# Graph attention over 8192 nodes: two edges packed in a byte before the adjacency is transposed, the packing by GpSimd, the unpacking by ScalarE, the row of neighbour terms in PSUM

## The reference

```python
h  = relu(layernorm(x))                     # x: 8192 x 128, float32
Wh = h @ W                                  # W: 128 x 128
f1 = Wh @ a[:128];  f2 = Wh @ a[128:]
e  = leaky_relu(f1[:, None] + f2[None, :], negative_slope=0.2)
e  = where(adj == 0, -inf, e)               # adj: 8192 x 8192, int32, about 0.2% ones
x + softmax(e, axis=1) @ Wh                 # float32
```

## Time and profile before

| | us |
|---|---|
| median of 3 runs (lowest, highest) | 870.19 (869.23, 870.61) |
| profiled execution, its span | 872.21, 870.5 |
| PE busy, DVE busy | 841.6 (97%), 766.2 (88%) |
| POOL busy, ACT busy | 137.0 (16%), 104.8 (12%) |
| transfers: mean rate | 87 GB/s written |

### The profile page before, as it was taken

How to read it: one execution, slowest core, us unless ns; L and a number is a source line. 1 busy time by engine, 2 the same in 40 slices (tenths; PEclk the granted TensorE clock), 3 DMA queues, 4 the chain that set the end, 5 groups by cost and what they waited for, 6 DMA issues and landing times.

```text
span 870.5 us, 23030 instructions
## 1 busy us (share of the span) xinstructions
PE 841.6 (97%) x9481; PEld 773.6 (89%) x9481; DVE 766.2 (88%) x1326; ACT 104.8 (12%) x286; POOL 137.0 (16%) x262
## 2 busy tenths in 40 slices
PE   3899999999999999999999999999999999999995
PEld 3788999999999999999999999999999999999995
DVE  4899898998989898898989889898989889898985
ACT  4788700000000000000000000000000000000000
POOL 3111111111111111111111111101110111111000
PEclk9999999999999999999999999999999999999998
DMA  9995699988998889888988998898889889988300
GB/s 219 113 107 52 59 112 87 94 92 80 95 91 90 83 91 95 81 92 87 97 83 90 91 85 92 81 103 83 90 83 94 92 81 94 93 90 82 48 2 15
DMA packets 43275, 75.95 MB, mean 87 GB/s; under 512 B 4720, under 2 KB 6896, under 8 KB 43248
## 3 DMA queue, kind: packets, MB, share of 16 engines
q0 software_dynamic: 38400, 67.13, 81.3%
q1 hardware_dynamic: 4432, 8.39, 2.9%
q10 hardware_dynamic: 416, 0.07, 0.0%
HBM read 272.70 MB, written 4.19 MB: 318 GB/s over the span
## 4 chain that ended last, share of the span: by engine, by line
PE 91%; DVE 6%; ACT 1%; DMA 1%; issue 1%; ACTq 0%; DVEq 0%
PE acc L275 50%; PE acc L279 26%; PE stage L264 13%; DVE wt_ring L620 3%; PE stage L237 1%; DVE stats L556 1%; DMA a_sb<-in_L_gnn_a_dram 1%; PE stage L224 1%; DVE pairs L611 1%; PE stage L252 1%; DVE xn L593 0%; ACT xn L399 0%; ACT wh L414 0%; DVE packed L603 0%; DVE xm L726 0%
## 5 line engine op out<-in xcount | busy, mean ns | idle before, releaser
L620 DVE SCALAR_TENSOR_TENSOR wt_ring<-row,packed,stage 128x512 f32<-128x512 uint8 (+1 forms) x1024 | 695.3, 742 | 74.9 <-PE acc L279 69.1
L275 PE MATMUL acc<-pairs,wt_ring 128*128 128x258 f16 x4096 | 720.2, 274 | 0.4 <-DVE wt_ring L620 0.2
L279 PE MATMUL acc<-pairs,wt_ring 128*128 128x129 f16 x4096 | 698.4, 219 | 0.0
L275 PEld LDWEIGHTS acc<-pairs,wt_ring 128*128 128x128 f16 x4096 | 396.2, 97 | 55.4 <-DVE wt_ring L620 0.4
L279 PEld LDWEIGHTS acc<-pairs,wt_ring 128*128 128x128 f16 x4096 | 399.5, 98 | 4.9
L178 POOL DMA_DIRECT2D masks<-in_adj_dram x252 | 133.2, 529 | 664.7 <-PE stage L264 635.7
L264 PE MATMUL stage<-ident,masks 128*128 128x128 f32 x1024 | 155.3, 275 | 2.0 <-ACT fin L483 2.0
L264 PEld LDWEIGHTS stage<-ident,masks 128*128 128x128 f32 x1024 | 108.7, 141 | 6.0 <-ACT fin L483 2.3
L513 ACT ACTIVATE fin<-acc 128x258 f32<-128x258 f32 x64 | 24.7, 386 | 730.2 <-PE acc L275 730.2
L237 PE MATMUL stage<-wx,ht 128*128 128x130 f32 x128 | 23.5, 311 | 0.7 <-ACT ht L408 0.7
L434 ACT ACTIVATE tmp<-wh,tmp 128x128 f32<-128x128 f32 x64 | 20.4, 390 | 0.4
(11 more groups left out here) (51 smaller groups left out, 80.1 us busy)
## 6 DMA issues: line engine op xcount, KB each, us to landing
masks<-in_adj_dram POOLq DMA_DIRECT2D x256, 256.0 KB, 8.8
out_dram<-xm SPq DMA_DIRECT2D x16, 256.0 KB, 2.1
xm<-in_x_dram SPq DMA_DIRECT2D x3, 1024.0 KB, 15.7
xm<-in_x_dram SPq DMA_DIRECT2D x1, 768.0 KB, 6.5
xm<-in_x_dram SPq DMA_DIRECT2D x1, 256.0 KB, 3.0
wx<-in_L_gnn_W_dram ACTq DMA_DIRECT2D x1, 64.0 KB, 3.2
a_sb<-in_L_gnn_a_dram ACTq DMA_DIRECT2D x1, 1.0 KB, 6.5
```

The lines of the kernel that those rows point to most:

```text
L275: return nc.tensor.matmul(acc[:, r, 0:2 * E1], wtv[:, w, r, 1, :], pairv[:, t, :, 0:E1], start=st, stop=end)
L279: return nc.tensor.matmul(acc[:, r, 0:E1], wtv[:, w, r, 0, :], pairv[:, t, 0, 0:E1], start=False, stop=False)
L620: nc.vector.scalar_tensor_tensor(out=wt_ring[:, t % NW, :], in0=e_row, scalar=packed[:, t, 1:2], in1=marks[:, k, :], op0=ALU.max, op1=ALU. ...
```

## The change

Rows 2 and 3 of each partition are multiplied by 200 and added to rows 0 and 1, so that one byte holds two edges (0, 1, 200 or 201). Only two blocks are then transposed per unit. The parts:

- **GpSimd** does, for each unit, `second` (the multiplication, on 128 x 2 x 256 16-bit words) and `mix` (the addition, on 128 x 2 x 128 32-bit words, which waits for `second` by a semaphore). It also takes over `scaled` and the second half of `normalise` in the first group, and `sums` and `outputs` of each group. Its loop is written out flat; it is ahead of PE by four to eight units.
- **ScalarE** does `unpack` for each unit: the bytes in PSUM times 1.28 plus 0.1, written as 16-bit integers into the ring `marks` of four units, so that the two bytes of each are the two edges. It also does `divided` (four 128 x 128 scalings) per group. `keep_row` is gone.
- **VectorE** reads E from PSUM (`stage`, bank 1 or 3) and the edges from SBUF (`marks`). `finish` is gone but for one reciprocal per group. It copies four columns of E for the next group into `e_next`.
- **TensorE** spreads E once per group, after unit 2, into the bank that is free, and transposes two units ahead into banks 0 and 2 in turn (before three ahead, over four banks).
- Loads: a chunk's rows 0 and 1 are loaded again when it is transposed, rows 2 and 3 when they are mixed. In the first group the loads of chunks 1 to 3 stand behind `second` and `mix` of units 0 to 3.

```diff
+            def mix(u):
+                c, k = u // KC % NC, u % KC
+                if k == 0 and u >= KC:
+                    pool.wait_ge(adj_loaded[c], (u // UN + (1 if c else 0)) * 2 * 16)
+                pool.wait_ge(s["second_pool"], u + 1)
+                sl = slice(k * P, (k + 1) * P)
+                nc.gpsimd.tensor_tensor(edges4[:, c, 0, :, sl], edges4[:, c, 0, :, sl], edges4[:, c, 1, :, sl],
+                                        ALU.add).then_inc(s["mixed"], 1)
+            def second(u):
...
+                nc.gpsimd.tensor_scalar(twos[:, c, 1, :, sl], twos[:, c, 1, :, sl], SECOND, None, ALU.mult
+                                        ).then_inc(s["second_pool"], 1)
+            def load_second(n):
+                pool.wait_ge(s["mixed"], (n - NC + 1) * KC)
...
+            def load_first(n):
+                pool.wait_ge(s["transposed"], (n - NC + 1) * KC)
...
+            def sums(q):
+                pool.wait_ge(s["acc_free"], (q + 1) * PACK)
...
+            for u in range(KC):
+                second(u)
+                mix(u)
+            for c in range(1, NC):
+                load_rows(c)
+            load_second(NC)
+            for b in range(UN):
+                if b % KC == 2:
+                    load_first(NC + b // KC)
+                if b + 1 < NQ:
+                    scaled(b + 1)
+                if b + 4 < NQ:
+                    normalise(b + 4)
+                second(b + KC)
+                mix(b + KC)
+                if b % KC == KC - 1:
+                    load_second(NC + 1 + b // KC)
+            for n in range(NC - 1, NQ * NC - 2):
+                if NC <= n < NQ * NC - NC:
+                    load_first(n + NC)
+                for k in range(KC):
+                    second((n + 2) * KC + k)
+                    mix((n + 2) * KC + k)
+                if n + 2 + NC < NQ * NC:
+                    load_second(n + 2 + NC)
+                if n >= NC and n % NC == 0:
+                    sums(n // NC - 1)
+                if n >= NC and n % NC == 2:
+                    outputs(n // NC - 1)
-                for r in range(PACK):
+                pe.wait_ge(s["mixed"], u + 1)
+                for r in range(2):
+                    mm = nc.tensor.transpose(stage[:, bank, r * P:(r + 1) * P], words[:, c * PACK + r, kk * P:(kk + 1) * P],
+                                             ident[:])
                 mm.then_inc(s["transposed"], 1)
+            def group(q, bank):
+                for b in range(UN):
+                    pe.wait_ge(s["marked"], q * UN + b + 1)
+                    transposes(b % 2 * 2, (b + 2) % UN, q * UN + b + 2)
                     unit(q * UN + b, b, q)
+                    if b == 2:
+                        pe.wait_ge(s["weighted"], q * UN * PACK)
+                        pe.wait_ge(s["e_ready"], q + 2)
+                        spread(bank)
+            def unpack(bank, u, b):
+                act.wait_ge(s["transposed"], u + 1)
...
+                nc.scalar.activation(split[:, b % MR, :].rearrange("p (s w) -> p s w", s=PACK),
+                                     stage[:, bank, 0:BANK // 2].bitcast(U8).rearrange("p (w s) -> p s w", s=PACK),
+                                     ACT.Copy, scale=SPLIT, bias=ABOVE).then_inc(s["marked"], 1)
-                marks = stage[:, bank, :].bitcast(U8).rearrange("p (w s) -> p s w", s=PACK)
+                edges = marks[:, b % MR, :].rearrange("p (s w h) -> p s h w", s=PACK, h=2)
+                e_row = stage[:, bank, :].rearrange("p (h k) -> p h k", h=2)
                 for k in range(PACK):
                     t = b * PACK + k
-                    nc.vector.scalar_tensor_tensor(out=wt_ring[:, t % NW, :], in0=e_row,
-                                                   scalar=packed[:, t, 1:2], in1=marks[:, k, :],
+                    nc.vector.scalar_tensor_tensor(out=wtq[:, t % NW], in0=e_row,
+                                                   scalar=packed[:, t, 1:2], in1=edges[:, k],
                                                    op0=ALU.max, op1=ALU.mult).then_inc(s["weighted"], 1)
```

More of the change, by code:

```diff
@@ L64, in gat_kernel @@
     NW = 8
+    MR = 4
     HALF = PACK // 2
@@ L88, in gat_kernel @@
         pairs = sb("pairs", [P, NB, 2 * WC], F16)
-        row = sb("row", [P, N], F32)
+        marks = sb("marks", [P, MR, CHUNK], U8)
         wt_ring = sb("wt_ring", [P, NW, BANK], F32)
@@ new lines, in normalise @@
+            def normalise(g):
+                pool.wait_ge(s["ln_ready"], batch_of(g) + 1)
+                pool.wait_ge(s["xt_ready"], g - 1)
+                for r in range(HALF, PACK):
+                    t = g * PACK + r
+                    ins = nc.gpsimd.tensor_scalar(xn[:, g % 2, r * P:(r + 1) * P], xm[:, g, r * P:(r + 1) * P],
+                                                  small[:, 5, t:t + 1], small[:, 6, t:t + 1], ALU.mult, ALU.add)
+                ins.then_inc(s["xn_pool"], 1)
@@ L189, in _, with outputs, load_rows @@
+            def outputs(q):
+                pool.wait_ge(s["fin_scaled"], q + 1)
+                y = xm[:, q, :].rearrange("p (r k) -> p r k", r=PACK)
+                nc.gpsimd.tensor_tensor(y, fin[:, :, 0:Fo], y, ALU.add).then_inc(s["rows_done"], PACK)
+            def load_rows(c):
                 pool.wait_ge(x_loaded[c + 1], 16)
@@ L191, in _ @@
                     load(0, c, r)
-            with pool.Fori(1, NQ) as q:
-                for c in range(NC):
-                    pool.wait_ge(s["transposed"], (q - 1) * UN + (c + 1) * KC)
-                    for r in range(PACK):
-                        load(q, c, r)
+            for u in range(KC):
[27 more added lines that the diff above has]
+                    outputs(n // NC - 1)
+            outputs(NQ - 2)
             pool.wait_ge(s["flag_ready"], 1)
@@ L309, in _ @@
             features(0, 1)
-            spread(0)
-            transposes(0, 0, 0, first=True)
+            transposes(0, 0, 0)
+            pe.wait_ge(s["e_ready"], 1)
+            spread(1)
             features(1, 0)
@@ L485, in _ @@
             for b in range(UN):
-                if b + 1 < NQ:
-                    scaled(b + 1)
+                if b + 1 < UN:
+                    unpack(0, b + 1, b + 1)
                 if b + 3 < NQ:
@@ L627, in first_weights, with next_group @@
                 if b == 0:
[L628 to L629 removed]
+                    dve.wait_ge(s["rowp_ready"], 1)
+                dve.wait_ge(s["marked"], b + 1)
                 if b >= 2:
                     dve.wait_ge(s["used"], b - 1)
[L632 removed]
+                weights(1, b)
+            def next_group(q):
+                dve.wait_ge(s["rowp_ready"], q)
+                nc.vector.tensor_copy(e_next[:], packed[:, bass.ds(q * PACK, PACK), 0]).then_inc(s["e_ready"], 1)
             nc.vector.memset(cst[:, 0:1], float(math.log(SCALE))).then_inc(s["cst_ready"], 1)
@@ L706, in _ @@
             nc.vector.tensor_scalar(lim[:, 1:2], low[:], -1.0, None, ALU.mult).then_inc(s["limits_ready"], 1)
-            dve.wait_ge(s["row_ready"], NQ)
-            with dve.Fori(1, NQ) as q:
-                rows(q)
+            with dve.Fori(0, (NQ - 2) // 2) as p:
+                rows(p * 2 + 1, 3)
+                rows(p * 2 + 2, 1)
+            rows(NQ - 1, 3, more=False)
             dve.wait_ge(s["limits_turned"], 1)
```

219 lines of the change are left out of this document (119 added, 100 removed).

## The result

| | before | after |
|---|---|---|
| median (lowest, highest), 4 runs each | 870.34 (869.23, 870.61) | 928.24 (925.82, 931.66) |
| ratio, 95% interval | | 1.0671 [1.0634, 1.0708] |
| profiled execution, its span | 872.21, 870.5 | 931.66, 930.0 |

The forecast was 827 us, the range 814 to 868, and faster had 0.86. The time lies above even the upper bound that the GpSimd rival gave (924 us).

A forecast was written before the change was run, and what follows sets the result against it. PE's instruction list was taken as the bound, with the DVE circle level with it: 870.5 us less 44.1 for groups 1 to 15, first group 0, gives 826.4, with half a microsecond for the tail 827 us; range 814 to 868.

The forecast's parts named there:

- the GpSimd rival: GpSimd's queue of packing and load issues becomes the bound above 2.93 us per unit; 924 us at 3.35; chance 0.24.
- GpSimd's price: GpSimd's work per unit: `second` 0.82 us, `mix` 0.82, with loads, wait, `sums` and `outputs` 2.64 us in all.
- upper bound of 2.19: Highest GpSimd cost considered, 2.19 ns per element from the select on 128 elements, giving 3.35 us per unit.
- margin of 0.29: GpSimd's forecast 2.64 us per unit against PE's 2.93, taken to fit by 10%.
- 240 c: Time of the later groups if GpSimd is the bound and a unit there takes c us.
- the sign: First sign of GpSimd as bound: DVE's reciprocal waiting for `sums`, forecast to end at 15.5 us, wanted at 17.6.
- The first group: Net change of the first group taken as 0, between -5 and +12 us; losing more than gaining had chance 0.06.
- The late start: In the first group, loads behind packing put `high_part(1)` at about 37.7 us, 8 late, 5 to 6 us lasting.
- A pass: First-group pass on DVE: 4.94 us to 4.4, 0.5 saved on 12 passes and some on the last four, 8 us.
- The rival of GpSimd and DVE blocking each other: DVE instructions with two SBUF tiles wait for GpSimd, 13 us, 840 us; weights, one SBUF tile, not held; chance 0.1.
- PE's list: PE's own instructions: two transposes fewer, 2.906 us per unit, and `spread` 0.44 us, 46.94 us per group against 50.02.
- the circle with DVE: DVE and PE waiting on each other across units: 2.908 us per unit, slack zero, no cost at today's DVE durations.

The follow-up runs named there:

- e6: The kernel after with PE's fourteen middle groups written out instead of looped, all else as after: 899.45 us, ratio 1.0341.
- e5: e1 with PE's fourteen middle groups written out, no jump back: 841.41 us, ratio 0.9662.
- e9: e5 with loads of chunks 1 to 3 ahead of the packing of units 1 and 2, and `scaled(1)` on ScalarE: 834.10 us, ratio 0.959.
- e8: e5 with loads of chunks 1 to 3 ahead of packing units 1 and 2, `scaled(1)` on ScalarE, `second` on ScalarE from unit 8: 832.66 us.
- e3: The kernel after with VectorE's reciprocal after unit 9 instead of 6 and the scalings after unit 11 instead of 8: 893.88 us, ratio 1.0258.
- e7: The kernel before with PE's loop body made two groups long, same instructions: 896.11 us, ratio 1.0290.
- e1: The kernel after with `second` moved from GpSimd to ScalarE from unit 20 on, six units ahead: 878.33 us, ratio 1.0090.

## Why the prediction was wrong

By medians, from after back to the forecast, in this order: PE without the long loop body -28.8 (e6); `second` off GpSimd -58.0 (e5); the start of the first group -7.3 (e9); `second` off GpSimd in the first group -1.4 (e8). That is 95.6 of the 101.2 us between 928.2 and 827. The other 5.7 us are in point 5. The shares depend on the order: the loop body was worth 37 us once GpSimd was out of the way.

1. **GpSimd's price, the step that failed most.** The prediction took 0.10 us fixed and 1.4 ns per element read, and so 0.82 us for `second`. It is 1.50 us, 2.9 ns per element, above even the upper bound of 2.19. `mix` on 512 elements read was 0.73 (0.82 forecast), `sums` 1.54 + 1.10 (2.36), `outputs` 1.20 (1.53). So of the computing instructions only the `tensor_scalar` was put too low, and it stood 256 times: 0.68 us per unit, against a margin of 0.29 (2.93 - 2.64). The rows used were of other instructions (memset, select) of at most 128 elements. The Trainium skill (GPSIMD Engine Reference, Performance versus the Vector engine) has the instruction with one input as the cheaper; the trace disagrees: 1.53 us for 516 float32 with one input, 1.10 with two. Its 2.6 cycles of 1.2 GHz per element for `tensor_tensor` agree with the 1.10 us.
2. **The rival's sum was short too.** It was 240 c; with c = 3.16 that gives 878 us. The groups took 2.5 us more than that list, because DVE's queue stands still at the reciprocal, PE behind it and, with the stop of point 3, GpSimd's loads behind PE. The prediction named the sign and gave it no price; taking away one of the two stops gives back 29 (e6) or 34 us (e3).
3. **PE's loop body, not foreseen.** The prediction counted PE's instructions per unit and not per pass. The clue was in the diff, a body of two groups for the two banks; no row of before showed a price. It is 25 us on the kernel before (e7) and 37 in e1, where PE is the bound too (e5).
4. **The first group: +15.1 against 0 (-5 to +12).** The late start was placed right (37.7 forecast, 38.01 measured), but more of its 8 us lasted, 7.3. A pass was to become 0.5 us shorter (4.94 to 4.4) and became 0.47 longer: from the second L747 to the last, fourteen passes, it is 5.87 us on the mean, before (L611) 5.41 (some passes are longer than the 4.94 that the prediction read). That is 6.6 us. Part of it is `scaled` on GpSimd, for which ACT waited nine times, 16.5 us in all, 9.4 of them the late start. The rival of GpSimd and DVE blocking each other was real there too. DVE's groups from 38 us to the end of the first group, before and then after (columns as in the earlier trace rows):

```profile
L611 DVE SCALAR_TENSOR_TENSOR pairs<-pairs,tmp 128x516 f16<-128x516 f16 x14 | 9.7, 691 | 0.0
L593 DVE TENSOR_SCALAR xn<-xm,small 128x128 f32<-128x128 f32 x22 | 6.6, 340 | 0.0
...
L603 DVE SCALAR_TENSOR_TENSOR packed<-exps,packed 128x8 f16<-128x8 f32 x13 | 2.2, 171 | 0.4
L602 DVE TENSOR_SCALAR packed<-exps 128x8 f16<-128x8 f32 x13 | 2.1, 165 | 4.5 <-ACT tmp L427 4.4
```

```profile
L747 DVE SCALAR_TENSOR_TENSOR pairs<-pairs,tmp 128x516 f16<-128x516 f16 x15 | 13.7, 915 | 5.4 <-ACT pairs L582 5.3
L738 DVE TENSOR_SCALAR packed<-exps 128x8 f16<-128x8 f32 x14 | 7.8, 554 | 4.5 <-ACT tmp L537 4.5
L739 DVE SCALAR_TENSOR_TENSOR packed<-exps,packed 128x8 f16<-128x8 f32 x14 | 7.7, 549 | 0.5
L700 DVE TENSOR_TENSOR small<-stats 128x16 f32<-128x16 f32 x2 | 3.0, 1504 | 0.0
```

   14 x 0.39, 14 x 0.38, 15 x 0.22 and 2 x 1.3 (0.19 before) make 17 us of holding, more than the 6.6 us of `normalise` that DVE was rid of. The prediction had 0.41 us a pass for it, at a chance of 0.1, and named for the first group only instructions that read two tiles of SBUF; L738 reads one and is held as well. How the 6.6 us split between this and `scaled` stays open: no run takes GpSimd's work out of the first group, and e8, with `second` gone from unit 8 on, still ends it 7.1 us late.
5. **What was right.** PE's list and the circle with DVE: 46.94 us per group forecast, 46.9 in e5 and e8, where nothing else binds. The weight instruction kept its 742 ns, `unpack` took 1.02 us (0.93, at most 1.14), both hidden. The weights, with one tile in SBUF, were not held by GpSimd, as the argument against that rival said (they are 92% of DVE's work, 696.5 of 760.1 us, not 96). e8 is 5.7 us above the forecast: its first group 7.1, its other groups -2.6 (821.88 - 118.32 = 703.6 against 706.2), and 1.2 lies outside the groups.

## What to carry to other kernels

A move of work to an idle engine is bounded by what that very form of instruction costs there at that size; where no row shows it, the upper bound isn't an upper bound, and an engine that would be 90% full by a guess is the likeliest to become the bound. When a loop body grows, look at its length per pass for each engine, not only at the work per unit. And two stops that each cost little beside a full engine can cost 30 us together: place a step that waits for another engine (here the reciprocal) late enough in its queue.

## What was not expected of the hardware

- With a loop body of 1,096 matmuls and transposes PE stops for 3.7 us at each jump back (e1), and the granted clock is at half (0.53) behind it; a jump costs 5.6 us in e1, 4.2 in e7. With a body of 576 the groups of before show no such stop.
- GpSimd's `tensor_scalar` is slower than its `tensor_tensor`: 512 uint16 in 1.50 us, 516 float32 in 1.53 against 1.10. ScalarE does the 512 uint16 in 0.62 us.
- A VectorE instruction of 128 x 8 elements (0.17 us before the change) took up to 1.6 us beside GpSimd, and ended when GpSimd's instruction ended.
